# Graph layers with a bitonic edge sort: falling runs held as negatives, turns in halves, and the first normalisation moved to ScalarE

## What is computed

```python
src, dst = both sorted by dst
h = maximum(layernorm(x), 0); x = x + L0(h)   # attention, softmax over the edges of one src, sum over dst
h = maximum(layernorm(x), 0); x = x + L1(h)   # attention with edge features, softmax over dst
h = maximum(layernorm(x), 0); x = x + L2(h)   # graph attention, softmax over dst
h = maximum(layernorm(x), 0); x = x + L3(h)   # weighted sum of neighbours, two products
# in L0:
key, query, msg = x_i @ Wk + bk, (x_j @ Wq + bq) / sqrt(32), x_j @ Wm + bm
alpha = segment_softmax(sum(query * key), by=src) * count(src)
out = segment_sum(msg * alpha, by=dst)
```

## Time and profile before

| | |
|---|---|
| median of 3 runs | 12159.75 us (12159.68 to 12168.47) |
| the profiled execution, its own time | 12157.44 us |
| its span, first to last instruction | 12155.7 us |
| busy: VectorE, ScalarE, GpSimd, PE | 62%, 44%, 68%, 12% |
| sort and normalisation, to the write of the sorted keys | 0 to 656 us |
| tables, masks, node counts | 656 to about 940 us |
| the five passes and the ends of the layers | about 940 to 12155 us |

### The profile page before, as it was taken

The page is one execution under the profiler, slowest core; times in us unless marked ns, Lnnn a source line. Parts: engine busy times, 40 slices in busy tenths (PEclk is TensorE's granted clock), DMA queues, the critical chain, the costliest instruction groups (busy, mean ns, idle before and its releaser), DMA issues.

```text
span 12155.7 us, 59249 instructions
## 1 busy us (share of the span) xinstructions
PE 1455.4 (12%) x5450; PEld 1244.1 (10%) x5450; DVE 7516.9 (62%) x7339; ACT 5311.8 (44%) x5435; POOL 8285.0 (68%) x8734
## 2 busy tenths in 40 slices
PE   2104544445100000021000000200000000000001
PEld 1103444444100000010000000200000000000001
DVE  8734555555288888857999999544444553333333
ACT  1034444444166666634666666333333333333332
POOL 1037777777577777756777777577777767777776
PEclk7555555555555555555555555555555555555555
DMA  4735666666366666635666666233333333333333
GB/s 167 268 101 184 203 205 206 204 202 206 91 213 211 215 214 211 213 119 179 214 214 214 214 214 214 75 111 110 113 112 110 112 90 100 106 106 106 103 106 103
DMA packets 795658, 1963.17 MB, mean 162 GB/s; under 512 B 214907, under 2 KB 423251, under 8 KB 794914
## 3 DMA queue, kind: packets, MB, share of 16 engines
q1 hardware_dynamic: 461770, 1140.56, 26.5%
q0 software_dynamic: 333856, 822.30, 23.9%
HBM read 1220.42 MB, written 741.78 MB: 161 GB/s over the span
## 4 chain that ended last, share of the span: by engine, by line
DVE 27%; POOL 24%; issue 21%; DMA 10%; ACT 8%; PE 7%; SPq 1%; DVEq 1%; ACTq 0%; POOLq 0%
POOL region L1158 22%; DVE work L1306 8%; DMA region<-start_rows_by_src 5%; DVE psB L1214 4%; PE psR L1073 3%; PE psR L1074 3%; ACT work L1389 3%; DMA region<-x,ix_s 2%; DVE work L1242 2%; DVE psR L1246 2%; DVE region L563 2%; DVE psR L1299 2%; DVE region L564 2%; ACT psB L1337 2%; POOL work L1559 1%
## 5 line engine op out<-in xcount | busy, mean ns | idle before, releaser
L1306 DVE TENSOR_TENSOR_SCAN work<-work,psR 128x1792 f32<-128x1792 f32 (+2 forms) x496 | 1971.5, 3975 | 91.7 <-DVE ix_s L1229 56.0
L1324 ACT COPY work<-region 128x1664 f32<-128x1664 f32 (+1 forms) x496 | 1166.6, 2352 | 1892.4 <-DMA region<-start_rows_by_dst 964.4
L1214 DVE TENSOR_TENSOR_SCAN psB<-psB,work 128x1792 f32<-128x1792 f32 (+1 forms) x496 | 1485.2, 2994 | 695.3 <-ACT psB L1337 629.5
L1158 POOL DMA_INDIRECT region<-kv,ix_s x1612 | 1524.1, 945 | 568.2 <-issue 455.2
L1158 POOL DMA_INDIRECT region<-qm,ix_s x1612 | 1524.5, 946 | 526.2 <-issue 454.9
L1158 POOL DMA_INDIRECT region<-x,ix_s x1612 | 1521.1, 944 | 528.8 <-issue 458.6
L1158 POOL DMA_INDIRECT region<-k,ix_s x1612 | 1521.4, 944 | 521.0 <-issue 514.0
L1158 POOL DMA_INDIRECT region<-h,ix_s x1612 | 1521.2, 944 | 491.4 <-issue 490.8
L1389 ACT COPY work<-work 128x1664 f32<-128x1664 f32 (+3 forms) x620 | 1573.8, 2538 | 0.0
L1388 ACT COPY psR<-work 128x128 f32<-128x128 f32 (+2 forms) x496 | 190.3, 384 | 2627.5 <-DVEq L1307 2627.5
L1242 DVE TENSOR_TENSOR work<-region,psB 128x1664 f32<-128x1664 f32 x372 | 702.4, 1888 | 563.9 <-DMA work<-keyrow,row_i 382.0
(11 more groups left out here) (296 smaller groups left out, 5909.6 us busy)
## 6 DMA issues: line engine op xcount, KB each, us to landing
region<-start_rows_by_dst SPq DMA_DIRECT2D x248, 832.0 KB
state_p<-work SPq DMA_DIRECT2D x124, 936.0 KB
state_p<-work SPq DMA_DIRECT2D x124, 884.0 KB
start_rows_by_src<-zero_t SPq DMA_DIRECT2D x1, 103168.0 KB, 275.4
region<-start_rows_by_src SPq DMA_DIRECT2D x124, 832.0 KB
start_rows_by_dst<-zero_t SPq DMA_DIRECT2D x62, 1664.0 KB, 8.0
state_pA<-work SPq DMA_DIRECT2D x124, 832.0 KB
state_p<-work SPq DMA_DIRECT2D x124, 832.0 KB
```

Of the source, the lines that this page charges most:

```text
L1158: g_.indirect_dma_start(rows_s[b][:, k, 0:wd_s], None, q.tabs, bass.IndirectOffsetOnAxis(ap=ix_s[b][:, k:k + 1], axis=0))\
L1214: nc.vector.tensor_tensor_scan(near_ps[:, 0:m], near_ps[:, 0:m], zt[:, 0:m], 0.0, ALU.mult, ALU.add).then_inc(q.s("held"), 1)
L1306: c.do(nc.vector.tensor_tensor_scan(st[:, 0:F * (K + 1)], decay_at(q, b)[:, 0:F * (K + 1)], summed[:, 0:F * (K + 1)], 0.0, ALU.mult, ALU.add))
L1324: nc.scalar.copy(f_by_t(zt, q.HF)[:, :, 1:K + 1].rearrange("p f t -> p t f"), rows_d[b][:, :, :].rearrange("p t w -> p (t w)")[:, 0:K * q. ...
```

## The change

- Keys of falling runs are held multiplied by -1 from the start: `keys_dve` multiplies odd and even elements of each key array by two sign columns (four `tensor_scalar` of 1024). A stage is then always min and max of the whole width. The sign flips only on the first stage of each k or round: `scalar_tensor_tensor` with scalar -1 takes -other against held, four instructions of 512 (or two of 1024 where nothing falls).
- The first sort reads `keyin[0]` in place, without its way through DRAM; `keyin[0]` later serves as `uppers`.
- Turns go in halves. PE transposes eight blocks into `sum_ps` (psR) once VectorE's half is done, ScalarE copies one operand's half to `uppers`, VectorE reads the other operand from PSUM and `uppers` from SBUF. The sign products at L610, L618, L622 and the copy at L582 are gone. The last stage before a turn is issued in two parts, so that the first half can be turned while the second is computed.
- The normalisation of layer 0 is on ScalarE (`norm0_act`): per block one Identity with a sum and one Square with a sum, then Sqrt; the normalised and clipped block is one Relu with scale and bias per partition, written straight to `hst`. VectorE does only the reciprocal and one product (`beside_sort_dve`), issued inside the sort after k = 7, with `flag_dve` and the small products for `w_2` there as well.
- The 13 projection groups are unrolled and use two output tiles (`tab` and a piece of `work`), so ScalarE waits for the tables of two groups before.

```diff
+            for o in range(2):
+                for h in range(2):
+                    a = keyin[o].rearrange("p (n h) -> p h n", h=2)[:, h]
+                    q.did(nc.vector.tensor_scalar(a, a, sgn[:, h:h + 1], None, ALU.mult))
...
-            for o in range(2):
-                sp.dma_start(keys_dram[o], keyin[o]).then_inc(S("keys_out"), 16)
-            sp.wait_ge(S("keys_out"), 32)
+            sp.dma_start(keys_dram[1], keyin[1]).then_inc(S("keys_out"), 16)
+            sp.wait_ge(S("keys_out"), 16)
...
+            b = Keys(X if o else keyin[0])
...
+            def order(to, lo, hi):
+                q.did(nc.vector.tensor_tensor(to[0], lo, hi, ALU.min))
+                q.did(nc.vector.tensor_tensor(to[1], lo, hi, ALU.max))
+
+            def flip_order(to, held, other):
+                q.did(nc.vector.scalar_tensor_tensor(out=to[0], in0=other, scalar=-1.0, in1=held, op0=ALU.mult, op1=ALU.min))
+                q.did(nc.vector.scalar_tensor_tensor(out=to[1], in0=other, scalar=-1.0, in1=held, op0=ALU.mult, op1=ALU.max))
...
+            def last_by_halves():
+                for h in range(2):
+                    order(pairs(turn_half(b.oth, h), 0), *pairs(turn_half(b.cur, h), 0))
                 b.swap()
...
             for k in range(1, LOGC):
...
+                flip_signed(b.oth, b.cur, b.cur, k - 1)
+                b.swap()
+                q.wait()
+                for j in reversed(range(k - 1)):
+                    stage(j)
+                if k == 7 and not o:
+                    beside_sort_dve(v)
+            flip_plain(b.oth, b.cur, b.cur, LOGC - 1)
...
+            for lp in range(1, LOGP + 1):
+                for h in range(2):
+                    turned(h)
+                    (flip_signed if lp < LOGP else flip_plain)(turn_half(b.oth, h), turn_half(sum_ps, h), turn_half(uppers, h), lp - 1)
+                b.swap()
+                q.wait()
+                for j in reversed(range(1, lp - 1)):
+                    stage(j)
+                if lp > 1:
+                    for y in range(2):
+                        to, a = turn_quarters(b.oth, y), turn_quarters(b.cur, y)
+                        order((to[:, 0], to[:, 1]), a[:, 0], a[:, 1])
                     b.swap()
...
+                for y in range(2):
+                    turned(y)
+                    order([turn_quarter(b.oth, 2 * x + y) for x in range(2)], turn_quarter(sum_ps, y), turn_quarter(uppers, 2 + y))
...
+            for turn in range(len(turn_steps)):
+                back, lp = turn % 2, turn // 2 + 1
+                for h in range(2):
+                    act.wait_ge(S("sort_turns"), o * SORT_TURNS + 2 * turn + (2 if back and lp == 1 else h + 1))
+                    if back:
+                        to, a = turn_quarter(uppers, 2 + h), turn_quarter(sum_ps, 2 + h)
+                    else:
+                        to, a = pairs(turn_half(uppers, h), lp - 1)[1], pairs(turn_half(sum_ps, h), lp - 1)[1]
+                    nc.scalar.copy(to, a).then_inc(S("sort_uppers"), 1)
...
+                for h in range(2):
+                    pe.wait_ge(S("sort_steps"), o * SORT_STEPS + steps[h])
+                    for c in range(C // P):
+                        if (c // 4 % 2 if back and lp > 1 else c // 8) == h:
+                            ins = nc.tensor.transpose(sum_ps[:, c * P:(c + 1) * P], keys[:, c * P:(c + 1) * P], ident[:, :])
+                    ins.then_inc(S("sort_turns"), 1)
...
+        def beside_sort_dve(v):
+            flag_dve(v)
+            q = line(v)
+            v.wait_ge(S("sqrt0"), 1)
+            q.do(nc.vector.reciprocal(ln_a[:, 2, :], ln_a[:, 3, :]))
+            q.do(nc.vector.tensor_tensor(ln_a[:, 0, :], ln_a[:, 1, :], ln_a[:, 2, :], ALU.mult))
+            v.sem_inc(S("ln0_by_dve"), 1)
...
+            for j in range(NB):
+                nc.scalar.activation(unread[:, j, :], xsb[:, j, :], ACT.Identity, accum_out=ln_a[:, 0, j:j + 1]).then_inc(S("ln0_sums"), 1)
...
+            for j in range(NB):
+                nc.scalar.activation(unread[:, j, :], xsb[:, j, :], ACT.Square, bias=ln_a[:, 1, j:j + 1],
+                                     accum_out=ln_a[:, 2, j:j + 1]).then_inc(S("ln0_sums"), 1)
...
+            def normed(g):
+                for j in range(BPG):
+                    n = g * BPG + j
+                    ins = nc.scalar.activation(hst[:, j, :], xsb[:, n, :], ACT.Relu, scale=ln_a[:, 2, n:n + 1], bias=ln_a[:, 0, n:n + 1])
+                ins.then_inc(S("h0_group"), 1)
+
+            normed(0)
+            for g in range(NG):
                 act.wait_ge(S("tr0"), g + 1)
                 nc.scalar.copy(hT[:, 0, :], psA[:, :]).then_inc(S("ht0"), 1)
...
+                if g < NG - 1:
+                    normed(g + 1)
                 act.wait_ge(S("mm0"), g + 1)
...
+                if g > 1:
+                    act.wait_ge(S(f"j0_out{g % 2}"), 48 * (g // 2))
+                nc.scalar.copy(tab0[g % 2], psB[:, :, 0:3 * D]).then_inc(S("raw0"), 1)
```

More of the change, by code:

```diff
@@ L131, in graph_layers_kernel @@
         nid = sb("nid", [P, NB])
-        sgn = sb("sgn", [P, 8])
+        sgn = sb("sgn", [P, 2])
+        eps_t = sb("eps_t", [P, 1])
         wcat0 = sb("wcat0", [P, 3 * D])
@@ L398, in padding_dve @@
             nc.vector.memset(next_i[:, :], PADN).then_inc(S("padded"), 1)
+            nc.vector.memset(eps_t[:, :], EPS).then_inc(S("padded"), 1)
             nc.vector.memset(ctz[:, :], 0.0).then_inc(S("dummies"), 1)
@@ new lines, in sort_pe @@
+        def sort_pe(pe, o):
+            n = sum(range(1, LOGC + 1))
+            for turn, steps in enumerate(turn_steps):
+                back, lp = turn % 2, turn // 2 + 1
+                n += 0 if turn == 0 else lp if back else LOGC
+                keys = Y if n % 2 else X
+                for h in range(2):
[4 more added lines that the diff above has]
+                    ins.then_inc(S("sort_turns"), 1)
```

263 lines of the change are left out of this document (108 added, 155 removed).

## The result

| | before | after |
|---|---|---|
| median of 5 runs | 12159.75 us | 12082.15 us |
| the runs | 12159.3 to 12168.5 | 12106.74, 12047.54, 12082.15, 12097.46, 12028.75 |
| the profiled execution, own time and span | 12157.44, 12155.7 us | 12106.74, 12105.0 us |
| sorted keys written at | 655.85 us | 524.73 us |
| gathers of the first pass (pB), first to last issue | 947.8 to 3065.2, 2117.4 us | 815.5 to 3007.4, 2191.9 us |

The medians are 77.6 us apart, a ratio of 0.994; the ratio over all the runs is given as 0.992, with a 95% interval of 0.9899 to 0.9941. The kernel is faster by some 78 us, not by 131, and its runs scatter over 78 us where those of before scatter over 9. The fastest of them is 12028.75 us, the forecast's time; the median lies 30 us above the end of the range.

The account below looks back on a forecast made before the run. The sort, bound by VectorE in its directed stages and by turns in its rounds, was what tables and passes wait for. 56.7 - 2.6 + 6.6 + 2.1 + 42.4 + 25.2 = 130.4 us off gave 12029 us, range 12012 to 12052.

Parts of the forecast that it names:

- Front: Before the sort: it starts at 34.4 instead of 91.12 us, behind four sign products of 2.4 us; +56.7 us.
- Stages: Sort stages on VectorE: full-width ones take 2.39 us against 2.53 for directed ones; together +6.6 us.
- Forward turns: Seven turns in the sort's rounds, done in halves: 4.7 us each instead of about 10.7; +42.4 us.
- turns back: Seven turns back in the rounds: 4.6 us instead of 8.3, 5.3 at lp = 1; +25.2 us.
- Projections: Beside the sort: root at 70 to 108 us, 13 groups of 7.3 us ending near 203; taken as 0.
- halves do overlap: Rival, sort turns: engines take the halves one after the other, 34 us more, 12063 us; 6%.
- the projections are not late: Rival, projection loop: groups at 12 us make the first turn wait 23 us, 12052 us; 5%.
- the clock is no faster: Rival, PE in the turns: denser turns raise the clock to 2.4 GHz, 1.5 us 14 times, 12008 us; 4%.
- Everything behind it moves up whole: Behind the sort: the five passes keep their length, so the sort's 130.4 us come off the whole time.
- more than 24 us away from 11500: Sign of being wrong: span from the sorted keys' write to the end more than 24 us from 11500.
- the passes lose their step: Slower rival, five passes: moved tensors and gather start cost 0.21 us or more in 620 steps; 12185 at 0.25; 2%.
- Nothing in the rows shows a dependence of that kind: Argument against the slower rival: no row shows passes depending on tensor placement or start moment; their instructions are the same.

Follow-up runs that it names:

- E9: Kernel after, with the halves of every turn of the sort put one behind the other; 12069.1 us, sorted keys at 565.1 us.
- E15: Kernel before, with eight late copies (24.5 us) once on ScalarE ahead of pB's loop; 12267.3 and 12273.75 us.
- E13: Kernel before, with four late copies (12.2 us) once on ScalarE ahead of pB's loop; 12156.48 us.
- E17: E15 with SyncE's zero chunk issued behind the first load of start rows in each double-step; 12149.27 us.
- E16: E10 with eight late copies once on ScalarE ahead of pB's loop; 11996.33 us.
- E14: Kernel after, unchanged, on a chip with 12158.06 us for before; 12028.39 us.
- E10: Kernel after, each load of start rows issued half a double-step sooner and pB's zero chunk moved behind both loads; 11988.96 us.
- E18: Kernel after, each load of start rows issued half a double-step sooner, zero chunk left in place, on a chip with 12174.5 us for before; 12007.63 us.

## Why the prediction was right about the sort and wrong about the time

*The sum.* 130.4 us were to come off ahead of the sorted keys' write, at 525.4; it stands at 524.73, 131.1 us earlier.

- Front: 35.51 for 34.4, a miss of 1.1 us: the keys began at 19.59 and not, as taken, at 18.84, and the four sign products took 2.74 us for 2.4.
- Stages: the full-width directed ones take 2.40 us, as taken from the earlier trace rows.
- Forward turns 4.5 us for 4.7, turns back 4.5 for 4.6; at lp = 1, 5.8 for 5.7 and 5.2 for 5.3. E9 prices their overlap at 40 us, where the rival had 34.
- Projections: no wait for the square root (68.95 for a bound of 70 to 108), ScalarE's last copy for them ends at 182.9 for 203 (a group took 5.9 us, not 7.3, off the path), the first turn's transposes come at 239.31 for 239. The additions' stretch is 13 x 3.1 us, as before (13 x 3.2).
- The rivals: halves do overlap (4.5 us a turn), the projections are not late (the first turn at 239.31), and the clock is no faster (0.54 in the rounds against 0.53).

That the sum is off by only 0.7 us is in part luck: the last stage before the first turn ended at 240.46 for 239.2, 1.3 us late, and the rounds took 2 us less than forecast.

*The step that failed* is "Everything behind it moves up whole". It moved up whole to pB's first gather and in four passes out of five. In pB 39 of the profiled execution's double-steps went from 34.3 to 36.2 us, which is nearly all of the 74.5 us that it lost, and its end took 8.6 more. From the sorted keys to the end it is 11580 us, where the prediction had named more than 24 us away from 11500 as a sign of being wrong. The nearest thing in the prediction is the slower rival, "the passes lose their step": right that passes can lose step, wrong in its size (0.21 us or more in all 620 steps, where it was 0.95 us in 78 of them) and in its sign, since no run of the changed kernel was slower than before. Its sentence "Nothing in the rows shows a dependence of that kind" was true of the rows that were read. It was not true of the trace: the 33.7 us of GpSimd's issue, the chain's 34.3 and a lag that climbs from 24.6 to 31 us could have been read before the run. The slow double-step of 36.2 us could not; with its 1.9 us more the range would have reached up to 12029 + 62 x 1.9 + 9 = 12156.

*What is shown.* Pass pB has two rhythms. The slow one holds itself to the end of the pass once it is there (E15 against before). The fast one takes back 3.8 us of lag (E13) and doesn't take back 16 (E15), but it doesn't hold for certain: the profiled execution of after left it after the 21st double-step with no push that the trace names. The slow one rests on the longer load behind the zero chunk (E17), and it doesn't hold when loads come early (E16). It does not need the change: E15 has none of it. Nor does the change always bring it: E9 and E14 have the change's placement, E14 is the changed kernel itself, and the five executions of the two show no sign of it, two of them in their traces and the others by their times.

*What stays open.* What tips the kernel after so often on the first chip: four of its five runs lie 19 to 78 us above 12029, and that those without a trace tipped as well, at other double-steps, is inferred from their times alone. The kernel before seems to tip as well, late or briefly: 12168.47, 12167.99 and 12192.21 us are single executions among others within 5 us of 12158; they were not traced. On the first chip the load took 10.4 to 11.6 us at lags above 31, in the traces of E9, E13 and E14 9.5 to 11.1 at lags of 31 to 32.7; so the edge may lie elsewhere from chip to chip. The placement was bounded only on chips where the slow rhythm always holds; before with the shift was never timed on a fast one. What GpSimd waits for in the pause is open as well. Which transfer makes the load late behind the key-row gather (the gather's own rows, or the pay rows and the chunk that then meet GpSimd's next ones) wasn't separated. The Trainium skill, "DMA: Bandwidth & Descriptors", section "Queues, rings and completion order", says that each of the sixteen engines takes turns between the queues that have work, a packet at a time, and that on each engine the descriptors of one queue are consumed in order. By that the load shares with whatever GpSimd has just issued, and the chunk ahead of it in SyncE's own queue comes first. E17 agrees with the second half (7.0 us for the load ahead of the chunk); for the first there is only the 12.1 against 9.8 us.

## What to carry to other kernels

When two engines pace a loop within a few per cent of each other (33.7 and 34.3 us here), read how their distance moves over the whole loop, not only the mean of a step: a lag that climbs and hovers says that one engine is held to the other, and here the kernel was one disturbance away from another time. A load should be issued as soon as its buffer is free and ahead of bulk traffic that nobody waits for; in this kernel that is worth 40 us at best speed (E10's 11989 against E14's 12028, on two chips with 12158 us for before), and E10's four executions lie within 2 us; it was not run on the first chip. And a forecast that "everything behind moves up whole" needs such a look at what is behind.

## What the runs showed of the hardware

- One delay of ScalarE, 8 us at GpSimd, cost 112 us (E15 against before), and 7 us in a kernel whose loads are early (E16 against E10).
- GpSimd's pause of 1 to 2.8 us after the same gather (the fifth behind the key row's) in every fourth double-step of before grows with the lag (0.3 us at 28.6, 3.4 at 33.0) and is absent from E10, E17 and E18. So it is no fixed cost of the gathers but a wait, which the trace shows as "issue".
- The same 832 KB load took 7.0 us from issue to its reader when it was issued ahead of a 1.7 MB store on SyncE's queue (E17), 10.0 behind it (before), and 11.9 behind it and behind GpSimd's gather of the key row (after).
- The same kernel before took 12158, 12174.5 and 13827 to 13891 us on different chips. On the last, pB's double-step went from 34.3 to 43 us and the last pass from 2011 to 2229, with the same busy time per instruction (a gather 944 to 946 ns in all). The sort took the same time on all of them (keys at 654 to 657 us, or 523 to 526 in the kernels with the change's sort).
